# Turning the token rows of an expert tile: on TensorE from one load, or on VectorE from four loads in 256-byte runs

## What is computed

```
x = x + attn(layernorm(x))          # attn: a Mamba block with its own norm and residual
x = x + ffn(layernorm(x))           # ffn: a mixture of 8 experts, 2 of them for each token

logits = x @ Wg + bg                # 8 experts
topk_w = softmax(top_k(logits, 2))
h   = relu(x @ W1[e] + b1[e])       # 256 -> 512
eo  = h @ W2[e] + b2[e]             # 512 -> 256
y   = sum over the 2 experts of topk_w * eo, plus x
out = layernorm(y) * gamma + beta
```

## Time and profile before

| | us |
|---|---|
| median of 3 runs | 2424.22 |
| the runs | 2422.47, 2424.22, 2425.36 |
| span of the profiled execution | 2425.2 |
| its stretch up to the first tile load (Mamba block, routing, tables) | 1846.0 |
| from there to the first product of the last tile | 504.7 |
| from there to the end (drain, load back, last norm) | 74.5 |

### The profile page before, as it was taken

How to read it: one execution, slowest core, us unless ns; L and a number is a source line. 1 busy time by engine, 2 the same in 40 slices (tenths; PEclk the granted TensorE clock), 3 DMA queues, 4 the chain that set the end, 5 groups by cost and what they waited for, 6 DMA issues and landing times. The chain is left out here.

```text
span 2425.2 us, 47399 instructions
## 1 busy us (share of the span) xinstructions
PE 2186.3 (90%) x13721; PEld 1766.3 (73%) x13722; DVE 2038.4 (84%) x3037; ACT 1506.5 (62%) x3292; POOL 1827.8 (75%) x1093
## 2 busy tenths in 40 slices
PE   8889899998989898998989898999787999999980
PEld 5667677677777666777777776767676999999970
DVE  5999999999999999999999999999974555555558
ACT  6687877878786877878787878877741111111106
POOL 3888989889898989889888989898962434444447
PEclk9999999999999999999999999999987999999995
DMA  5041322314041323324041413223137998999978
GB/s 172 7 134 54 131 75 102 124 52 164 21 158 48 131 69 114 106 70 153 32 156 34 144 49 135 80 96 116 62 123 199 226 228 229 229 230 229 229 166 277
DMA packets 186791, 312.50 MB, mean 129 GB/s; under 512 B 18851, under 2 KB 118083, under 8 KB 186500
## 3 DMA queue, kind: packets, MB, share of 16 engines
q1 hardware_dynamic: 140932, 258.53, 33.4%
q0 software_dynamic: 25584, 34.62, 7.5%
q10 hardware_dynamic: 20112, 17.32, 2.2%
HBM read 247.09 MB, written 63.32 MB: 128 GB/s over the span
## 5 line engine op out<-in xcount | busy, mean ns | idle before, releaser
L855 POOL TENSOR_TENSOR dbu<-drive_u,b_rows 128x1024 f32<-128x1024 f32 x384 | 904.3, 2363 | 87.7 <-DVE ps_a L660 35.1
L1159 ACT ACTIVATE ps_a<-delta,a_neg 128x512 f32<-128x512 f32 x768 | 517.2, 685 | 136.9 <-DVE ss L660 120.2
L872 POOL TENSOR_TENSOR wp<-ss,rows_c 128x1024 f32<-128x1024 f32 x192 | 453.6, 2363 | 37.6 <-DVE ss L660 36.9
L1766 POOL DMA_INDIRECT acc_scratch<-ow,idx x135 | 211.2, 1564 | 309.2 <-issue 102.4
L672 DVE TENSOR_TENSOR wd<-ps_a,rows_c 128x1024 f32<-128x1024 f32 x320 | 383.3, 1198 | 0.0
L1437 PEld LDWEIGHTS ps_y<-ident,wd 128*128 128x128 f32 x2560 | 299.4, 143 | 98.7 <-issue 70.5
L1437 PE MATMUL ps_y<-ident,wd 128*128 128x128 f32 x2560 | 337.3, 277 | 12.4 <-DVE wd L672 12.4
L1804 ACT COPY e_meta<-xt 128x2 f32<-128x2 f32 x135 | 25.9, 192 | 439.0 <-PE e_ps_x L1877 294.4
L1464 PEld LDWEIGHTS ps_a<-dg,duT 128*128 128x128 f32 x2048 | 248.6, 196 | 60.6 <-issue 58.1
L1464 PE MATMUL ps_a<-dg,duT 128*128 128x128 f32 x2048 | 259.0, 281 | 31.6 <-ACT carry L1166 28.6
L1688 DVE TENSOR_SCALAR e_hT<-e_ps_h,b_turned 128x128 f32<-128x128 f32 x540 | 152.1, 344 | 144.7 <-PE e_ps_h L1886 125.2
(11 more groups left out here) (200 smaller groups left out, 3653.8 us busy)
## 6 DMA issues: line engine op xcount, KB each, us to landing
b_rows<-in_L_ffn_W_dram SPq DMA_DIRECT2D x135, 512.0 KB
rows_c<-b_scratch SPq DMA_DIRECT2D x128, 512.0 KB, 4.9
b_rows<-b_scratch SPq DMA_DIRECT2D x96, 512.0 KB, 4.1
xt<-xs_scratch SPq DMA_DIRECT2D x135, 129.0 KB
xb<-in_L_attn_x_dram SPq DMA_DIRECT2D x16, 512.0 KB, 4.0
hx<-in_L_attn_x_dram SPq DMA_DIRECT2D x16, 512.0 KB, 6.3
x_scratch<-hx SPq DMA_DIRECT2D x16, 512.0 KB, 2.9
acc_scratch<-stage SPq DMA_DIRECT2D x16, 512.0 KB, 2.9
```

The lines of the kernel that those rows point to most:

```text
L855: pool.tensor_tensor(dbu[:, k % NBU], du[:, g % 2, :].unsqueeze(1).broadcast_to([P, 2, CH]), bb[:, row:row + 2, :], ALU.mult).then_inc(dbu ...
L872: pool.tensor_tensor(wp[:, s % 2], ss[:, s % 2], cc[:, rows, :], ALU.mult).then_inc(wp_done, 1)
L1159: act.activation(dst, dl[:, g, :], ACT.Exp, scale=a_neg[:, g, n:n + 1]).then_inc(exp_done, 1)
L1766: pool.indirect_dma_start(out=acc_dram, out_offset=bass.IndirectOffsetOnAxis(ap=idx[:, old, :], axis=0), in_=ow[:, old, :], in_offset=None ...
```

## The change

The token rows of a tile are no longer turned by TensorE. They load in such an order that VectorE, which can transpose each 32x32 block of a tile in one instruction, brings them into the form that the first product needs.

- The tile of 128 rows by 256 features is loaded with four transfers (i = 0 to 3). Transfer i takes features 64·i to 64·i + 63 of all rows, 256 bytes of each, and puts them onto partitions 32·i to 32·i + 31: row 32·j + b goes to partition 32·i + b, columns 64·j on. A fifth transfer brings the weight and the row number of each row, 8 bytes, into `xm`.
- VectorE transposes all of `xt` in one instruction into `xT`, at the head of its step, after waiting for the five transfers and for the first product of tile s − 2. After it, partition p holds features 2p and 2p + 1. To match, the first matrices load as `(p k)` and no longer as `(k p)`: one run of 4096 bytes for each partition, where there were two of 2048.
- TensorE has no identity products and ScalarE no copy of the turned rows any more. ScalarE copies the weight and the row number from `xm`. SyncE waits for VectorE (`x_turned`) and ScalarE (`meta_copied`) before it reuses a slot.

The diff, cut to what the steps touch; its pieces below the buffers are, in this order, of SyncE, VectorE (the transpose, then the row numbers), ScalarE and TensorE.

```diff
-        w1_t = W1.rearrange("e (k p) f -> p e k f", p=P)
+        w1_t = W1.rearrange("e (p k) f -> p e k f", k=KD)
...
+    QB = P // BLK
+    PARTS = QB + 1
...
-        xt = sb("xt", [P, RING, XW])
+        xt = sb("xt", [P, RING, QB, D // QB])
+        xm = sb("xm", [P, RING, 2])
-        xT = sb("xT", [P, 2, KD, P])
+        xT = sb("xT", [P, 2, QB, KD, BLK])
...
-                wait_apart(sync, passed, [(x_copied, 1, t, 1 - RING)])
-                sync.dma_start(xt[:, slot, :], xs_dram[bass.ds(off, P), :]).then_inc(t_in[slot], 16)
+                wait_apart(sync, passed, [(x_turned, 1, t, 1 - RING), (meta_copied, 1, t, 1 - RING)])
+                rows = xs_dram[bass.ds(off, P), :].rearrange("(j b) d -> b j d", b=BLK)
+                for i in range(QB):
+                    sync.dma_start(xt[i * BLK:(i + 1) * BLK, slot], rows[:, :, i * D // QB:(i + 1) * D // QB]
+                                   ).then_inc(t_in[slot], 16)
+                with nc.allow_non_contiguous_dma(reason="a weight and a row number for each row"):
+                    sync.dma_start(xm[:, slot], xs_dram[bass.ds(off, P), D:]).then_inc(t_in[slot], 16)
...
             def tile_step(s, slot):
                 par = slot % 2
+                if real(s):
+                    wait_slot(dve, t_in[slot], s, RING, slot, per=16 * PARTS)
+                    wait(dve, h_full, 1, s, -1)
+                    dve.transpose(xT[:, par], xt[:, slot].rearrange("p j (a k) -> p j k a", k=KD)).then_inc(x_turned, 1)
...
+                    wait(dve, meta_copied, 1, t, 1)
                     dve.tensor_tensor(idx[:, old, :], meta[:, old, 1:], aside[:, bass.ds(t, 1)], ALU.min
                                       ).then_inc(idx_done, 1)
...
                 if real(s):
-                    wait(act, x_turned, 1, s, 1)
+                    wait_slot(act, t_in[slot], s, RING, slot, per=16 * PARTS)
                     wait(act, o_weighed, 1, s, 1 - RING)
-                    act.copy(meta[:, slot, :], xt[:, slot, D:])
-                    wait(act, h_full, 1, s, -1)
-                    act.copy(xT[:, par].rearrange("p k n -> p (k n)"), ps_x[:, par, 0:KD * P]).then_inc(x_copied, 1)
+                    act.copy(meta[:, slot, :], xm[:, slot]).then_inc(meta_copied, 1)
...
-                if real(s):
-                    wait_slot(pe, t_in[slot], s, RING, slot)
-                    wait(pe, x_copied, 1, s, -1)
-                    for k in range(KD):
-                        ins = pe.transpose(ps_x[:, par, k * P:(k + 1) * P], xt[:, slot, k * P:(k + 1) * P], ident[:])
-                    ins.then_inc(x_turned, 1)
                 if real(s - 1):
                     t = s - 1
-                    wait(pe, x_copied, 1, t, 1)
+                    wait(pe, x_turned, 1, t, 1)
...
-                                            xT[:, 1 - par, k, :], start=(k == 0), stop=(k == KD - 1))
+                                            xT[:, 1 - par, :, k, :], start=(k == 0), stop=(k == KD - 1))
```

More of the change, by code:

```diff
@@ L18 @@
 W1_EARLY = 1
+BLK = 32
 def wait(eng, sem, per, c, k):
@@ L1573, in moe_block @@
         ow = sb("ow", [P, RING, D])
-        ps_x = ctx.enter_context(nc.psum_tensor("e_ps_x", [P, 2, CH], F32))
+        ps_n = ctx.enter_context(nc.psum_tensor("e_ps_n", [P, 2, CH], F32))
         ps_h = ctx.enter_context(nc.psum_tensor("e_ps_h", [P, 2, KF, P], F32))
@@ L1577, in moe_block @@
         ps_b = ctx.enter_context(nc.psum_tensor("e_ps_b", [P, 2, CH], F32))
-        sums = [ps[:, b] for ps in (ps_x, ps_h[:].rearrange("p b k n -> p b (k n)"), ps_o) for b in range(2)]
+        sums = [ps[:, b] for ps in (ps_n, ps_h[:].rearrange("p b k n -> p b (k n)"), ps_o) for b in range(2)]
         assert W == CH
@@ L1585, in moe_block @@
         x_turned = sem("x_turned")
-        x_copied = sem("x_copied")
+        meta_copied = sem("meta_copied")
         h_full = sem("h_full")
@@ L1799, in tile_step @@
             def tile_step(s, slot):
-                par = slot % 2
                 if real(s):
-                    wait(act, x_turned, 1, s, 1)
+                    wait_slot(act, t_in[slot], s, RING, slot, per=16 * PARTS)
                     wait(act, o_weighed, 1, s, 1 - RING)
-                    act.copy(meta[:, slot, :], xt[:, slot, D:])
-                    wait(act, h_full, 1, s, -1)
-                    act.copy(xT[:, par].rearrange("p k n -> p (k n)"), ps_x[:, par, 0:KD * P]).then_inc(x_copied, 1)
+                    act.copy(meta[:, slot, :], xm[:, slot]).then_inc(meta_copied, 1)
             def load_x1(i):
@@ L1832, in normalise @@
                 if c < SLOTS:
-                    act.wait_ge((x_copied, h_done, o_done)[b // 2], NTT)
+                    act.wait_ge((h_full, h_done, o_done)[b // 2], NTT)
                 else:
```

## The result

The changed kernel takes **2577.32 us** (median of 4 runs, 2576.53 to 2578.15) against 2424.79 (4 runs, 2422.47 to 2427.07): a ratio of 1.063, interval 1.061 to 1.064, slower. The prediction was 2609 in 2540 to 2680. The profiled execution has a span of 2576.4 us and took 2578.15.

A forecast was written before the change was run, and what follows sets the result against it. SyncE's in-order issues were to replace TensorE as the bound: 2.70 + 2.40 = 5.10 us a tile, putting the last first product 185.2 us later, so 2424.22 becomes 2609 us, range 2540 to 2680.

The forecast's parts named there:

- The bound: In the tiles, SyncE becomes slowest and waits for no one; DMA share under 0.9, TensorE idle some 1.7 us a tile.
- A piece at 0.60 us: SyncE's issue of one piece of the rows: 42 + 29 + 388 + 3·47 ns, 0.60 us.
- SyncE's base of 2.70 us: SyncE's work for each tile before the change, taken between about 2.6 and 2.83 us.
- The second wait, offset against a cheaper matrix load: On SyncE, the second semaphore wait adds about 0.06 us, the one-run matrix load loses about 0.05: nothing net.
- The sum: Last matrix load issued at 2531.8, landing 4.1 us later; last first product at 2535.9, 185.2 us later; tail 74.54 unchanged.
- The other engines: VectorE at most 2.7 us a tile, DMA engines 3.4 to 4.7, both hidden under SyncE's 5.1; ScalarE idle anyway.
- TensorE's saving of 0.32 us: Identity products removed from each tile on TensorE, leaving 3.41 us of work; worth 43 us if TensorE stayed the bound.
- the fourth rival: SyncE's issues run beside its other work, under 0.26 us for each added transfer: 2381 us, or about 2430; chance 0.04.
- Issuing between 0.35 and 0.45 (the first): Rival: a piece costs SyncE 0.35 to 0.45 us, a tile 4.0 to 4.6, time 2462 to 2542; chance 0.07.
- The small packets (the second): Rival: 256-byte packets cost 98 ns, the DMA engines bind at 6.2 us a tile, time 2756; chance 0.04.
- The clock (the third): Rival: TensorE, idle 1.7 us of each 5.1, is granted a lower clock, 0.67 seen at 62% busy; chance 0.03.
- One issue against one landing: An issue costs 0.41 to 0.60 us against 4.1 for a landing, but adds up in an in-order stream while landings overlap.

The follow-up runs named there:

- the run with the matrix form alone: Kernel before with only the first matrices' layout changed to one 4096-byte run a partition, identity products picking columns to match: 2425.58 us, ratio 1.0005.
- the one-load runs: Changed kernel with its four piece loads made one of 128 partitions: 2418.28 us with 512 packets of 256 bytes, 2418.03 with 128 of 1 KB.
- the split kernel: Changed kernel with three of four pieces and the weights and row numbers issued by ScalarE, one piece and the matrix by SyncE: 2416.85 us.
- both kernels that split by halves: Changed kernel with two loads of 64 partitions for four pieces, 2528.94 us; kernel before with its rows' load in two of 64 partitions, 2425.01.

## Why the prediction was right, step by step

- **The bound: right.** SyncE waits for no one, the DMA share is 0.79 (under 0.9 was said), the clock 1.00, TensorE waits for the matrix load. It idles 1.1 us a tile (22% of 4.88) where 1.7 was said: the tile is shorter, and TensorE's work in it larger, than the prediction had them (3.52 us by starts of products, not 3.41). With one extra issue the time stands still, with three it rises by the sum, and with the pieces moved to another queue the loss is gone.
- **A piece at 0.60 us: too dear.** It is 0.51, and the 0.55 to 0.65 named as a sign was missed. The instruction takes 332 ns where I took the matrix load's 388 "with the extra dimension", the register operation 37 for 42, and the three gaps about 36 ns each and not 47. Over four pieces that is 0.37 us a tile.
- **SyncE's base of 2.70 us: too low.** The tile of 4.88 less 2.03 for the pieces and the 0.06 that the prediction gave the second wait (its instruction takes 17 ns in the trace, with one gap of 36 to 47 that is 0.05 to 0.06) leaves 2.79. It was nearly the upper end, 3.73 less the measured waits, and no middle had to be chosen. That takes back 0.09.
- **The second wait, offset against a cheaper matrix load: nearly.** The load's instruction fell from 388 to 357 ns, 0.03; the 0.05 stands in the run with the matrix form alone (338).
- **The sum.** The last first product began at 2502.35, 33.5 us earlier than the 2535.9 of the sum. The tile makes 133 x (5.10 − 4.88), about 29.5 of it. Of the rest, 2.3 is the first piece going out at 1843.65 instead of 1846.0, which the change does not explain, 1.2 the time from there to the first matrix load (6.3 us, 5.10 + 2.4 in the sum), and 0.4 the last matrix landing in 3.7 us instead of 4.1. The tail was 74.05 us against 74.54.
- **The other engines: right where it mattered.** The transpose takes 0.445 us in bounds of 0.36 to 0.63, and is hidden. DMA work a tile is 0.79 x 4.88 = 3.9 us in bounds of 3.4 to 4.7.
- **TensorE's saving of 0.32 us: wrong, without effect here.** 0.32 was the time from one weight load to the next across the transposes. By starts of products a tile is 1.79 + 1.73 + 0.22 before, and the identity products are the 0.22. So the fourth rival's 2381 was out of reach: with 0.22 it is 2424 − 30 = 2394, and 2393 was measured once nothing else stood in the way. The same error is in my expectations of 2381. The starts, in the timeline of TensorE before:

```profile
1861.70 0.38 PE L1877 MATMUL e_ps_x<-ident,xt 128*128 128x128 f32 x2
1861.92 1.95 PE L1886 MATMUL e_ps_h<-xT,b_rows 128*128 128x128 f32 x16
1863.70 1.89 PE L1895 MATMUL e_ps_o<-rows_c,e_hT 128*128 x8
1865.43 0.38 PE L1877 MATMUL e_ps_x<-ident,xt 128*128 128x128 f32 x2
```

- **The rivals.** Issuing between 0.35 and 0.45 (the first) failed by little, 0.51. The small packets (the second) fell by the one-load runs. What such packets cost is to be read in the split kernel, where ScalarE's queue moves 75293 packets (a mix of 8, 256 and 1024 bytes, mean 253) in 22.7% of 420 x 16 us, 20 ns each, against the 98 that this rival assumed, twice the 49 of 1 KB. The clock (the third) stayed at 1.00 though TensorE idled for 22% of the stretch; no run here shows what a tile takes at a lower clock. The point of decision of the fourth, 0.26 us for each added transfer, was right in kind: at 0.51 SyncE could take one, not four.
- **One issue against one landing: right.** One transfer takes 0.51 us to issue and 2.7 to 3.9 to land, yet six issues and the table work of a tile, 4.88 us in all, were the bound. The size of the packets set no time here: 2418.28 us with 256-byte packets, 2418.03 with 1 KB, and the DMA share 0.97 against 0.93. Both kernels wait for the scatters, so they can't tell what small packets would cost where the DMA engines are the bound.

## What to carry to other kernels

Count, for each tile and for each queue that issues transfers, the sum of its issues and table work, and get its reserve from its waits: here 0.9 us a tile, one more transfer free, four of them 6% slower. An engine that no busy table lists can be the bound, and moving issues to an idle engine's queue can give the loss back without touching a transfer (2577.32 us to 2416.85 here). When one bound is lifted, price the next stream that has its own order (here scatters that wait for each other) before counting the gain, and test it with a kernel that makes that stream alone cheaper. Deeper buffers need not help where a rate is the limit: here eight in place of four filled up too, and the time was 2424.50 us against 2416.85.

## What was not expected of the hardware

- The time of the instruction that issues a transfer depends on its shape and hardly on its bytes: 351 ns for 1 KB (381 in the run with three extra transfers) and 338 for 129 KB on 128 partitions, and by shape 332 ns for 32 partitions of 4 runs, 608 for 64 of 4 runs, 477 for 64 rows of 1032 bytes, 389 for 128 partitions of 4 runs, 338 for 128 rows. In both kernels that split by halves, 64 partitions cost more than 32 or 128. Why is open; in the first of them the transfer that follows is slower too (463 ns against 351).
- Packets of 253 bytes in the mean take 20 ns, a quarter of the 84 ns of the main queue's 1578-byte mean: far less than a fixed price for each packet would give, though for each byte they are half as dear again.
- An indirect transfer that adds takes 2.7 times the DMA time of one that writes the same rows (24.8% of the engines for 114 against 9.6% for 120), and occupies GpSimd for 1.56 us instead of 0.96 (178.32 us for 114, 115.26 for 120).
